# One core, a selective scan in two directions: TensorE adds the softplus's logarithm onto PSUM, and the backward products are dealt nine to VectorE and seven to GpSimd

## The reference

```
dt  = softplus(dt @ dt_w.T + dt_b)              # 128 channels x 16384 tokens
dA  = exp(dt * A[s])                            # for each of 16 states s
dBx = dt * xc * B[s]
h   = dA * h + dBx                              # along the tokens, forward or flipped
y   = sum over s of h * C[s]  (+ xc * D)
y   = y * silu(z);  out = y @ out_w.T           # x += y_fwd + y_bwd
```

## Time and profile before

| | |
|---|---|
| median of three runs | 2513.69 us |
| profiled execution, its own time | 2513.28 us |
| its span (the other 3.0 us lie around it) | 2510.3 us |
| forward chunks (from 609.5 us) | about 52.4 us each |
| backward chunks (from 1448.3 us) | 53.6 to 54.8 us each |
| busy: TensorE, VectorE, ScalarE, GpSimd | 88%, 87%, 70%, 83% |

### The profile page before, as it was taken

The page is one execution under the profiler, slowest core; times in us unless marked ns, Lnnn a source line. Parts: engine busy times, 40 slices in busy tenths (PEclk is TensorE's granted clock), DMA queues, the critical chain, the costliest instruction groups (busy, mean ns, idle before and its releaser), DMA issues. The chain is left out here.

```text
span 2510.3 us, 37021 instructions
## 1 busy us (share of the span) xinstructions
PE 2198.3 (88%) x9158; PEld 1108.6 (44%) x9158; DVE 2172.0 (87%) x2247; ACT 1757.0 (70%) x3999; POOL 2075.0 (83%) x1330
## 2 busy tenths in 40 slices
PE   6899996866988999889999888989899889898698
PEld 6466664653444444444444333333343333343543
DVE  5677778355999999999999999999999999998796
ACT  4799998466787788877888756656556556553487
POOL 4466665114999999999999999999999999998499
PEclk9999997877999999999999999999999999989799
DMA  4000000015767667666677677777767777765022
GB/s 71 14 14 14 13 13 6 1 22 160 228 219 233 223 225 239 219 232 225 226 235 225 233 251 242 235 244 237 241 235 246 241 236 241 235 222 179 14 62 62
DMA packets 192552, 421.07 MB, mean 168 GB/s; under 512 B 66548, under 2 KB 95705, under 8 KB 192474
## 3 DMA queue, kind: packets, MB, share of 16 engines
q1 hardware_dynamic: 190938, 416.01, 52.3%
q10 hardware_dynamic: 1536, 4.20, 0.5%
HBM read 387.63 MB, written 24.12 MB: 164 GB/s over the span
## 5 line engine op out<-in xcount | busy, mean ns | idle before, releaser
L1592 POOL TENSOR_TENSOR s_hc<-s_h,s_cc 128x1024 f32<-128x1024 f32 x512 | 1200.4, 2363 | 58.7 <-PE s_py L1345 41.5
L1345 PE MATMUL s_py<-s_hc,ident 128*128 128x512 f32 x2048 | 983.2, 605 | 18.8 <-DVE s_yo L1638 18.4
L1675 DVE TENSOR_TENSOR_SCAN s_h<-s_dA,s_state,s_pu 128x1024 f32<-128x1024 f32 x330 | 770.5, 2342 | 27.7 <-PE s_pu L1323 4.7
L1345 PEld LDWEIGHTS s_py<-s_hc,ident 128*128 128x128 f32 x2048 | 387.2, 193 | 387.4 <-issue 310.7
L1506 ACT ACTIVATE s_dA<-s_dt,ss_A 128x1024 f32<-128x1024 f32 x352 | 401.6, 1142 | 9.1 <-ACT s_brow L1462 7.7
L1511 ACT ACTIVATE s_pu<-s_dt,ss_A 128x1024 f32<-128x1024 f32 x160 | 178.4, 1115 | 321.9 <-DVE s_h L1675 316.5
L1585 POOL TENSOR_TENSOR s_dbx<-s_dtx,s_bb 128x1024 f32<-128x1024 f32 x160 | 378.1, 2363 | 2.5 <-DVE s_dtx L1630 2.5
L1675 DVE TENSOR_TENSOR_SCAN s_h<-s_pu,s_state,s_dbx 128x1024 f32<-128x1024 f32 x150 | 350.3, 2335 | 22.2 <-ACT s_pu L1511 20.0
L1651 DVE TENSOR_TENSOR s_pu<-s_pu,s_dtx 128x1024 f32<-128x1024 f32 x288 | 349.3, 1213 | 15.7 <-PE s_pu L1332 13.3
L1332 PE MATMUL s_pu<-s_bcs,ss_sel 128*128 128x512 bf16 x576 | 177.8, 391 | 119.5 <-DVE s_h L1675 119.1
L591 POOL TENSOR_TENSOR ar_ex<-ar_ex,ar_rs 128x512 f32<-128x512 f32 x128 | 133.0, 1039 | 141.9 <-DVE ar_rs L538 141.8
(11 more groups left out here) (289 smaller groups left out, 3549.3 us busy)
## 6 DMA issues: line engine op xcount, KB each, us to landing
s_cc<-rows_scratch SPq DMA_DIRECT2D x512, 512.0 KB, 4.6
s_bb<-rows_scratch SPq DMA_DIRECT2D x160, 512.0 KB, 5.0
s_n<-n_scratch SPq DMA_DIRECT2D x64, 258.0 KB, 5.5
y_scratch<-s_yo SPq DMA_DIRECT2D x16, 512.0 KB, 5.5
s_yf<-y_scratch SPq DMA_DIRECT2D x16, 512.0 KB, 6.7
x_tok<-in_x_dram SPq DMA_DIRECT2D x16, 256.0 KB, 4.6
at_xg<-at_xT SPq DMA_DIRECT2D x64, 64.0 KB, 2.0
n_scratch<-ss_turned SPq DMA_DIRECT2D x32, 128.0 KB, 3.3
```

Source lines behind the costliest of these rows:

```text
L1345: ins = nc.tensor.matmul(p_y[:, hf], lhsT=c.ident[:, :], rhs=hc[:, s % RING, hf], start=(s == 0), stop=(s == U - 1))
L1592: nc.gpsimd.tensor_tensor(hc[:, s % RING, :], h[:, s % RING, :], cc[:, s % C_RING, :], ALU.mult).then_inc(read, 1)
L1675: nc.vector.tensor_tensor_scan(out=flow(h[:, s % RING, :]), data0=flow(decays), data1=flow(inputs), initial=begun, op0=ALU.mult, op1=ALU.a ...
```

## The change

GpSimd's addition of relu and logarithm goes. VectorE subtracts the correction from relu alone, and TensorE then adds `s_tb` onto the result in PSUM, with the identity as weights and `start=False`: two matmuls of 128x512, at unit 11. What follows goes one unit later: the copy of dt 11 to 12, `s_dtx` 12 to 13, the turning of x 13 to 14 with its copy 14 to 15, the projection 13 to 14, the addition to x 14 to 15. Backward, VectorE's ten products become nine (0, 1, 3, 5, 6, 8, 10, 12, 14) and GpSimd's six become seven (2, 4, 7, 9, 11, 13, 15). Seven is odd, so the waits on the two `s_bb` buffers are counted anew.

```
-             (0, 1, 3, 4, 6, 8, 9, 11, 12, 14))
+             (0, 1, 3, 5, 6, 8, 10, 12, 14))
...
+            def add_log(hf):
+
+                def step(w, m, par):
+                    pe.wait_ge(dt_summed, m + 1)
+                    pe.wait_ge(log_made, m + 1)
+                    ins = nc.tensor.matmul(p_p[:, hf], lhsT=c.ident[:, :], rhs=tb[:, hf], start=False, stop=True,
+                                           skip_group_check=True)
+                    if hf.start:
+                        ins.then_inc(sum_made, 1)
+                return step
...
-            shared = [(0, convolve(a)), (1, convolve(b)), (2, in_out(a)), (3, in_out(b))]
+            shared = [(0, convolve(a)), (1, convolve(b)), (2, in_out(a)), (3, in_out(b)), (11, add_log(a)), (11, add_log(b))]
...
-            tail = {forward: (), backward: [(13, project)]}
+            tail = {forward: (), backward: [(14, project)]}
...
             def take_dt(w, m, par):
-                act.wait_ge(dt_summed, m + 1)
+                act.wait_ge(sum_made, m + 1)
...
-                       (8, softplus_log), (9, part_middle), (11, take_dt)]
-            prepare = {forward: first + [(5, take_columns_b)] + rest_of + [(14, take_turned_x)],
+                       (8, softplus_log), (9, part_middle), (12, take_dt)]
+            prepare = {forward: first + [(5, take_columns_b)] + rest_of + [(15, take_turned_x)],
...
-            def linear_and_log(w, m, par):
-
-                pool.wait_ge(relu_made, m + 1)
-                pool.wait_ge(log_made, m + 1)
-                nc.gpsimd.tensor_tensor(tc[:, :], tc[:, :], tb[:, :], ALU.add).then_inc(sum_made, 1)
...
             def step_sum(w, m, par):
-                dve.wait_ge(sum_made, m + 1)
+                dve.wait_ge(relu_made, m + 1)
...
-            prepare = [(9, lost), (10, step_sum), (12, dt_x)]
-            tail = {forward: (), backward: [(LAG_SUM - 1, gate), (14, add_x)]}
+            prepare = [(9, lost), (10, step_sum), (13, dt_x)]
+            tail = {forward: (), backward: [(LAG_SUM - 1, gate), (15, add_x)]}
...
-                need(sp, g_injected, w.upto(G, n) + r + 1 - B_RING)
+                if r >= B_RING:
+                    sp.wait_ge(g_injected, w.upto(G, n) + r - B_RING + 1)
+                elif n:
+                    last = range(r, len(way_of(n - 1).g), B_RING)[-1]
+                    sp.wait_ge(g_injected, w.upto(G, n) - len(way_of(n - 1).g) + last + 1)
```

More of the change, by code:

```diff
@@ L1126, in upto, with spreads @@
         done = NC * (len(units(w.before)) // each) if w.before is not None else 0
+        return n * per + (done - w.start * per)
+    def spreads(self, n, slot):
+        w = self.of(n)
+        per = len(range(slot, len(w.g), B_RING))
+        done = NC * len(range(slot, len(w.before.g), B_RING)) if w.before is not None else 0
         return n * per + (done - w.start * per)
@@ L1391, in _ @@
             a, b = halves
-            shared = [(0, convolve(a)), (1, convolve(b)), (2, in_out(a)), (3, in_out(b))]
+            shared = [(0, convolve(a)), (1, convolve(b)), (2, in_out(a)), (3, in_out(b)), (11, add_log(a)), (11, add_log(b))]
             prepare = {
-                forward: shared + [(4, columns_b), (6, step_size(a)), (6, step_size(b)), (13, turn_x)],
+                forward: shared + [(4, columns_b), (6, step_size(a)), (6, step_size(b)), (14, turn_x)],
                 backward: shared + [(5, step_size(a)), (6, step_size(b))]}
-            tail = {forward: (), backward: [(13, project)]}
+            tail = {forward: (), backward: [(14, project)]}
             add = [(8, add_input(a)), (9, add_input(b))]
@@ L1400, in _ @@
             run(pe, unit, prepare.get, tail.get, own.get,
-                (convolve(a), convolve(b), step_size(a), step_size(b), in_out(a), in_out(b), columns_b, turn_x))
+                (convolve(a), convolve(b), step_size(a), step_size(b), in_out(a), in_out(b), columns_b, add_log(a),
+                 add_log(b), turn_x))
             for s in range(U - LAG_SUM, U):
@@ L1582, in inject @@
                     pool.wait_ge(dtx_done, n + 1)
-                pool.wait_ge(b_spread[r % B_RING], 16 * (w.upto(G, n, B_RING) + r // B_RING + 1))
+                pool.wait_ge(b_spread[r % B_RING], 16 * (w.spreads(n, r % B_RING) + r // B_RING + 1))
                 need(pool, scanned, w.past(G, n, s, lambda v: B_RING))
@@ L1605, in _ @@
             nc.gpsimd.memset(bcs[:, :, :], 0.0).then_inc(zeroed, 1)
-            prepare = [(8, part_rest), (9, linear_and_log), (10, part_low)]
+            prepare = [(8, part_rest), (10, part_low)]
             assert min(forward.g) >= INJECT_AHEAD
-            run(pool, unit, lambda w: prepare, begin=(linear_and_log, part_rest, part_low))
+            run(pool, unit, lambda w: prepare, begin=(part_rest, part_low))
             read_c(ALL - 1, U - 1)
```

## The result

| | before | after |
|---|---|---|
| time, median of four runs (lowest to highest) | 2513.9 us (2512.3 to 2515.2) | 2578.3 us (2576.5 to 2579.3) |
| ratio, 95% interval | 1 | 1.026 (1.0247 to 1.0273) |
| profiled execution, its span | 2513.3, 2510.3 us | 2578.8, 2577.0 us |
| one forward chunk (mean of 16) | 52.42 us | 52.68 us |
| one backward chunk (mean of 15) | 54.26 us | 58.34 us |

The kernel is 64.4 us slower; 2527 was predicted, with a range up to 2543. A chunk is counted from its first scan to the next chunk's first scan. The spans differ by 66.7 us: 3.2 of it stand before the first scan (612.72 against 609.54), 4.0 in the 16 forward chunks, 61.2 in the 15 backward chunks that are followed by another, and -1.7 behind the start of the last. So the mechanism has to be sought backward.

A forecast was written before the change was run, and what follows sets the result against it. Backward, GpSimd was taken as the bound: 863.2 + 15 x (0.6 + 0.8) + 1.5 = 885.7 us instead of 871.5, +14.2, less 0.5 at the start, +13.7 on 2513.28: 2527 us. Range for all 2508 to 2543, the forecast's own 2518 to 2537.

The forecast's parts named there:

- Row C, 0.6 us a chunk: Backward, GpSimd's read of state 14 waits for its late row C: 0.6 us in each of 15 chunks, bounds 0.3 to 1.0.
- The fit that the prediction took from the Trainium skill: Row loads: about 2.0 us plus bytes over 436 GB/s, 3.2 us for 512 KB; not relied on, as measured loads were slower.
- T: Backward, the start of GpSimd's read right behind the product of state 15, from which the prediction counted landings.
- TensorE's clock, 0.8 us a chunk: Backward, TensorE idles for late `s_bcs`, its passes slow, GpSimd waits for a total: 0.8 us a chunk, bounds 0 to 1.2.
- third rival: Backward, TensorE's clock stays low through the dense stretch, GpSimd waiting 4 us more a chunk: 2574 us, chance 0.06.
- second rival: Backward, the loads come in time, no read waits and TensorE's gap is too short to matter: 2506 us, chance 0.12.
- the first's: Rival that only row C is late backward and TensorE's new gap costs nothing: 2515 us, chance 0.20.
- The sum backward: GpSimd's work, the two waits in 15 chunks and 1.5 for the last chunk: 885.7 us instead of 871.5, +14.2.
- The wait of 4.31 us in the last chunk: GpSimd's wait in the last backward chunk, behind an idle TensorE at the gate; 0 to 4.3 expected after, taken 1.5.
- Forward, 0: Forward chunks: the addition removed from GpSimd is slack and TensorE's possibly later spread was taken to cost 0.
- the rival of +1 us a chunk: Forward, TensorE's later spread costs 1 us in each of 15 chunks on top of the forecast: 2542 us, chance 0.12.
- The prologue, -0.5: First chunk: L1624 no longer waits for GpSimd, but dt's copy waits for the logarithm's passes: -0.5 us, between -1.5 and +1.0.

The follow-up runs named there:

- e2: Changed kernel with the next backward chunk's first row B issued behind rows C(14), C(15) and the load of the parts: 2512.8 us, ratio 1.0000 to the kernel before.
- e8: Changed kernel with the two row B buffers used in strict turn across chunks, SyncE's order untouched: 2511.6 us, ratio 1.0002 to the kernel before.
- e3: Changed kernel with the next backward chunk's first row B issued behind row C(14), still ahead of the parts and C(15): 2542.5 us, ratio 1.0112.
- e13: Changed kernel with 20 filling products on TensorE ahead of its wait for the parts in backward chunks: 2558.8 us, ratio 1.0199 to the kernel before.
- e14: e3 with 8 filling products on TensorE ahead of its wait for the parts in backward chunks: 2515.7 us, ratio 1.0027 to the kernel before.

## Why the prediction was wrong

**Right.** Backward is GpSimd's, with 23 products before and after; the seventh state makes the load of the next row B wait for the product of state 15, and with it row C(14) and `s_bcs`; both become waits, row C's on GpSimd and `s_bcs` on TensorE behind the projection; VectorE bears its own wait. e2 and e8 show that without the late load there is no loss.

**Row C, 0.6 us a chunk: the step that failed first.** The term took the landing of 4.7 us from a pair of loads and an upper bound of 5.1. The burst is six loads, since row C(15) and the row B behind it were free by then and only stood in the queue, and the row C behind those came free with the first read, 2.3 us later: 6.1 us for this one (the second), and 2.4 us of wait. Holding the three followers alone gave 1.1. I listed what waits ahead of the needed load and not what is let go behind it. Missing: 1.8 us x 15 = 27 us.

The fit that the prediction took from the Trainium skill (DMA: Bandwidth & Descriptors, "Anatomy of one DMA — SWDGE (gpsimd) path") is stated there for one transfer issued by GpSimd; these loads are SyncE's, in a burst. Its 3.2 us for 512 KB, an estimate, is near the 3.4 us of the first of the burst, and far from the 6.9 us of the median of five; row C landed at T + 6.6, not by T + 4.55.

**TensorE's clock, 0.8 us a chunk.** The idle time was put at 3.8 us and was 5.0, since the parts landed at T + 7.3, not T + 5.8, and the bound of 1.2 us was for one slow phase behind a start at T + 5.8. The longer idle time is not what made the term larger: in e3, with 2 us of it, the totals cost as much. GpSimd waited at three reads a chunk, where my walk of TensorE's queue checked one. (Of the 15 gaps before, 11 are followed by slow passes, not quite the four in five that I gave.) Measured 1.9 us, and e13 and e14 show that 1.4 to 1.6 of it go when only the clock is kept up. I never asked which read is due while the passes are slow: the read of state 15 needs the very total that follows the first spread, and it waited 0.27 us in the chunk shown. The mechanism was right and mis-sized by 1.1 us x 15 = 16 us. My third rival, the clock low through the dense stretch, came near in time (2574 us) but by luck: the slow passes were over after the first total, and more than half the loss was row C. Its sum was also wrong: 15 x 4.6 + 1.5 + 863.2 - 871.5 is +62.2, not +60.7, so with the start 2575 us. And the range of 2508 to 2543 does not take in the second rival's 2506, as the text there says; it takes in the first's 2515.

**The sum backward.** From GpSimd's first to its last read of the way 871.5 us were measured, and 885.7 forecast. 27 + 16 more make 929; from the read at the first scan of the way to the end of the last four it now takes about 930:

```profile
1455.43 2.35 POOL L1605 TENSOR_TENSOR s_hc<-s_h,s_cc 128x1024 f32<-128x1024 f32 x1
...
2375.90 9.28 POOL L1605 TENSOR_TENSOR s_hc<-s_h,s_cc 128x1024 f32<-128x1024 f32 x4
```

(2385.18 less 1455.43 is 929.8. The two orders differ at the start of the way, so the stretches compare to within a product, and the agreement is no closer than that.) The wait of 4.31 us in the last chunk is gone altogether, where 1.5 was left for it in the sum.

**Forward, 0.** It was +4.0 us. I looked at TensorE's queue for it (the rival of +1 us a chunk) and not at VectorE's order, where a moved instruction had been hiding 0.2 us of a product ahead of its scan; the trace shows that, and the times do not prove that it is the 4.0 us.

**The prologue, -0.5.** It was +3.2. The logarithm's passes come behind an idle TensorE and run slowly (TensorE, then ScalarE, where the earlier trace rows had the copy at 602.89):

```profile
603.23 3.78 PE L1319 MATMUL s_pp<-s_tb,ident 128*128 128x512 f32 x4 [4.73 <-DVE s_pp L1637]
...
607.11 1.01 ACT L1476 COPY s_dt<-s_pp 128x1024 f32<-128x1024 f32 x1 [3.94 <-PE s_pp L1319]
```

The first scan starts at 609.9 to 613.8 us (mean 611.6) in the twelve profiles in which TensorE adds in the first chunk, and at 608.9 to 609.9 (mean 609.5) in the four in which GpSimd does: +2.1 us is the change's, the rest of the 3.2 is scatter.

What stays open: why the forward chunks of the runs differ by 0.1 to 0.4 us among themselves with the same forward code, and how the landing grows between three and six loads.

## What to carry to other kernels

When a ring's length stops dividing the number of its users, look at which instruction owns the slot that the first load of the next round takes, and at everything behind that load in its queue: what it holds back leaves in one burst, and each load in the burst lands late by those behind it as well. Price a wait of TensorE by what it does to the passes behind it and by which read needs those passes, not by its length. And before moving an instruction by a unit, see what its neighbours hid behind it.

## What the runs showed of the hardware that was not expected

- A row load of 512 KB landed 3.5 us after its issue with nothing right ahead of it, 3.4 as the first of six issued in 2.3 us, 6.1 as the second, and 8.5 as the last; with three loads in the burst `s_bcs` took 4.6 us instead of 6.2.
- Five microseconds of idle TensorE cost 1.4 us on the four passes behind (3.30 against 1.88 us), and two cost as much (3.39 in e3, behind the same projection); forty useless passes of 128 columns in that gap (4.73 us) kept the passes at 1.88 us, and the kernel was faster with them (a ratio of 1.0199 to the kernel before, against 1.0260).
- On VectorE a 128x1024 product takes 1.11 us from start to start ahead of an independent instruction and 1.31 ahead of the scan that reads it.
